# The mixer's product of e^k and v for groups 2 and 3: from VectorE in PSUM to ScalarE and GpSimd in SBUF

## The reference

```python
r = sigmoid(h @ W_r.T + b_r);  ek = exp(h @ W_k.T + b_k);  v = h @ W_v.T + b_v
td = exp(b_td);  g = exp(global_decay)
def step(carry, inputs):                    # over the 1024 tokens
    sa = ek_t * v_t + td * sa
    sb = ek_t + td * sb
    wkv = (g * ek_t * v_t + sa) / (g * ek_t + sb + EPS)
    inp_t = r_t * wkv
    mem = BETA * mem + inp_t - spike(mem - THRESH) * THRESH
    spk = spike(mem - THRESH)
```

## Time and profile before

| | |
|---|---|
| profiled execution, its own time | 566.38 us |
| its span | 564.4 us |
| median of the three runs | 566.53 us |
| mean granted TensorE clock | 0.955 of full speed |
| PE busy | 491.8 us (87%) |
| VectorE (DVE) busy | 436.7 us (77%) |
| ScalarE (ACT) busy | 348.3 us (62%) |
| GpSimd (POOL) busy | 328.7 us (58%) |

### The profile page before, as it was taken

One profiled execution on the slowest core, in us unless ns is written; L12 is line 12 of the kernel. 1 busy time (PEld: TensorE's weight loads), 2 busy tenths in 40 slices (PEclk: granted clock), 3 DMA queues, 4 the chain that ended last, 5 costly groups with the idle time before them and its releaser, 6 DMA issues. The chain is left out here.

```text
span 564.4 us, 11730 instructions
## 1 busy us (share of the span) xinstructions
PE 491.8 (87%) x4033; PEld 310.3 (55%) x4033; DVE 436.7 (77%) x1181; ACT 348.3 (62%) x1001; POOL 328.7 (58%) x255
## 2 busy tenths in 40 slices
PE   7650048999999999999989999999999989999995
PEld 6320013467777766443457777776544445667774
DVE  6899999889999875556898888885445686467775
ACT  4971004789999987632589999997555525533331
POOL 5860006999999998476999999993011274210000
PEclk9885559999999999999999999999999999999999
DMA  8400002211111112000031111111000000000000
GB/s 291 157 1 1 1 1 87 64 37 35 36 40 38 40 39 75 2 1 1 26 87 41 38 40 39 39 39 30 0 3 0 1 1 0 1 0 20 21 19 20
DMA packets 14832, 19.93 MB, mean 35 GB/s; under 512 B 2314, under 2 KB 8948, under 8 KB 14644
## 3 DMA queue, kind: packets, MB, share of 16 engines
q1 hardware_dynamic: 14484, 19.08, 12.4%
q10 hardware_dynamic: 288, 0.08, 0.1%
HBM read 8.94 MB, written 1.05 MB: 18 GB/s over the span
## 5 line engine op out<-in xcount | busy, mean ns | idle before, releaser
L516 ACT ACTIVATE prob<-psS,nmx 128x128 f32<-128x128 f32 x256 | 90.1, 378 | 17.3 <-DVE nmx L1112 17.3
L806 POOL TENSOR_TENSOR rn<-ssq,half 128x16 f32<-128x16 f32 x32 | 93.1, 2908 | 6.9 <-DVE ssq L1098 6.8
L798 POOL TENSOR_TENSOR ra<-ra,rb 128x512 f32<-128x512 f32 x64 | 80.6, 1278 | 1.0 <-DVE rb L1080 0.9
L653 POOL TENSOR_TENSOR rst<-mv,half 128x4 f32<-128x4 f32 x24 | 25.7, 1070 | 81.9 <-DVE mv L899 69.8
L1458 PE MATMUL psQK<-wqkv,hsA 128*128 128x512 f32 x128 | 61.2, 596 | 0.9 <-DVE hsA L1061 0.6
L516 ACT ACTIVATION_READ_ACCUMULATOR prob<-psS,nmx 128x1 f32 x256 | 55.4, 216 | 0.0
L1077 DVE TENSOR_TENSOR ra<-psQK,rope 128x512 f32<-128x512 f32 x64 | 43.9, 685 | 9.8 <-PE psQK L1458 9.3
L814 POOL TENSOR_TENSOR qkn<-ra,rn 128x512 f32<-128x512 f32 x32 | 49.5, 1548 | 2.5
L1112 DVE TENSOR_REDUCE nmx<-psS 128x4 f32<-128x512 f32 x64 | 41.0, 683 | 4.5 <-PE psS L1560 4.5
L634 ACT ACTIVATE gel<-psQK 128x512 f32<-128x512 f32 x32 | 19.1, 597 | 39.7 <-PE psQK L1774 39.7
L1080 DVE TENSOR_TENSOR rb<-psQK,rope 128x512 f32<-128x512 f32 x64 | 43.5, 680 | 0.0
(11 more groups left out here) (237 smaller groups left out, 1208.0 us busy)
## 6 DMA issues: line engine op xcount, KB each, us to landing
vAB<-vAB SPq DMA_DIRECT2D x62, 128.0 KB, 2.2
wqkv<-in_wqkv SPq DMA_DIRECT2D x2, 768.0 KB, 7.9
big<-in_x SPq DMA_DIRECT2D x4, 256.0 KB, 5.5
ropeb<-in_rope SPq DMA_DIRECT2D x1, 1024.0 KB, 6.5
big<-in_ew SPq DMA_DIRECT2D x2, 512.0 KB, 4.4
out<-big SPq DMA_DIRECT2D x4, 256.0 KB, 2.3
wmod<-in_wmod SPq DMA_DIRECT2D x2, 384.0 KB, 5.8
w<-in_w SPq DMA_DIRECT2D x2, 341.0 KB
```

The source lines that it names most:

```text
L516: act.activation(prob[:, k, :], psS[:, hb, c * P:(c + 1) * P], ACT.Exp, bias=nmx[:, k:k + 1], accum_out=sums[:, n % 2, k:k + 1]).then_inc( ...
L798: pool.tensor_tensor(o, o, rb[:, r], ALU.add).then_inc(s["sum_" + name], 1)
L806: pool.tensor_tensor(rn[:, :], ssq[:, :], half[:, :], ALU.pow).then_inc(s["rn_ready"], 1)
```

## The change

For groups 0 and 1 nothing changes. For groups 2 and 3 ScalarE copies v with its bias from PSUM into `ekv` in SBUF, ahead of `gek`; GpSimd multiplies it there by ek (`product`), product(2) behind quotient(0) and product(3) behind quotient(1); VectorE's multiply is left out, and its second scan and its numerator read `ekv` in SBUF instead of PSUM. VectorE's wait for the product stands behind the scan of ek.

```diff
@@ ScalarE, behind ek_ready
+                if g >= 2:
+                    act.wait_ge(s["kv_mm"], 2 * g + 2)
+                    act.activation(ekv[:, gsl(g)], psO[:, g % 2, :], ACT.Identity, bias=vec[:, V_BV:V_BV + 1]).then_inc(s["v_ready"], 1)
@@ GpSimd
+            def product(g):
+                pool.wait_ge(s["v_ready"], g - 1)
+                pool.wait_ge(s["ek_ready"], g + 1)
+                pool.tensor_tensor(ekv[:, gsl(g)], ekv[:, gsl(g)], ek[:, gsl(g)], ALU.mult).then_inc(s["ekv_ready"], 1)
...
                 if g == 1:
                     quotient(0)
+                    product(2)
                 elif g == 2:
                     quotient(1)
+                    product(3)
                     current(0)
@@ VectorE
-                ekvp = psO[:, g % 2, :]
-                dve.wait_ge(s["kv_mm"], 2 * g + 2)
+                ekvp = ekv[:, c] if g >= 2 else psO[:, g % 2, :]
                 dve.wait_ge(s["ek_ready"], g + 1)
-                dve.scalar_tensor_tensor(out=ekvp, in0=ekvp, scalar=vec[:, V_BV:V_BV + 1],
-                                         in1=ek[:, c], op0=ALU.add, op1=ALU.mult).then_inc(s["ekv_ready"], 1)
-                dve.wait_ge(s["ekv_ready"], g + 1)
+                if g < 2:
+                    dve.wait_ge(s["kv_mm"], 2 * g + 2)
+                    dve.scalar_tensor_tensor(out=ekvp, in0=ekvp, scalar=vec[:, V_BV:V_BV + 1],
+                                             in1=ek[:, c], op0=ALU.add, op1=ALU.mult).then_inc(s["ekv_ready"], 1)
+                if g < 2:
+                    dve.wait_ge(s["ekv_ready"], g + 1)
...
                 dve.tensor_tensor_scan(sbb[:, c], td, ek[:, c], ...).then_inc(s["sb_ready"], 1)
+                if g >= 2:
+                    dve.wait_ge(s["ekv_ready"], g + 1)
```

More of the change, by code:

```diff
@@ L186, in program @@
             xT_fill xT_evac
-            kv_mm num_ready ek_ready gek_ready ekv_ready sb_ready den_ready r_mm r_ready rcp_ready quot_ready cur_ready x_mixed
+            kv_mm num_ready ek_ready gek_ready ekv_ready v_ready sb_ready den_ready r_mm r_ready rcp_ready quot_ready cur_ready x_mixed
             dve dve_b act_own pool_own fallback fallback_b rope_ready tabs_phase tabs_ready z_ready hsA_ready
```

## The result

The changed kernel takes 568.79 us (median of 5 runs, 567.86 to 569.64), the kernel before 566.38 (5 runs, 565.90 to 566.98). The ratio is 1.0042, 95% interval 1.0027 to 1.0057: slower by 2.4 us, between 1.5 and 3.2.

What follows compares the result with a forecast made beforehand. Bound: the mixer's chain to VectorE's membrane passes, with GpSimd's queue 0.36 us behind VectorE. Current(0) at 37.32 plus 7.17 us of turns puts the last reciprocal at 44.5 against 41.91, +2.6: 569.1 us, range 567.4 to 570.8.

Steps and rivals of the forecast that it cites:

- Group 2's saving is eaten: VectorE, group 2: den(2) takes a turn before the numerator; reciprocal at 34.08 not 33.18, saving lost and 0.19 us more.
- Seven instructions in turn in group 3: Group 3: VectorE's two scans and numerator alternate with GpSimd's two currents, quotient(2) and den(3), 7.17 us in sum.
- rival A: Exclusion costs little for the new forms, only GpSimd's queue counts: last reciprocal +0.4 us, 566.9 us; chance 0.12.
- r is later: ScalarE: two copies of 0.66 us each delay r's release from 35.86 to 37.18, 1.32 us.
- The lead that the prediction calls a microsecond: ScalarE, group 3: V's matmul ends a microsecond ahead of the copy, so the copy does not wait.
- Product(3) hidden: GpSimd, between quotient(1) and current(0): product ends at 36.4, before 37.3, costing nothing; without that cover 1.26 us.
- Rival B: Not slower: ScalarE's copies don't reach r, current(0) stays at 36.00; without exclusion -0.9 us, 565.6 us; chance 0.05.
- a sign that the prediction itself had named for being wrong: ScalarE's r coming under 0.9 us later than before, where 1.32 was worked out.
- that case: With exclusion and undelayed r, current(0) at 36.00 plus 7.17 gives 43.2 for the last reciprocal, still +1.3 us.
- its other signs: Among them: both group 3 scans at 1.7 to 2.2 us; wrong if they keep 1.25 beside GpSimd's work.
- Rival C: TensorE's clock rises later against its work, slowing fillers after the passes: likely +1, 570.1, up to 570.8; chance 0.12.
- Rival D: VectorE's numerator at half rate with two SBUF sources: its 0.60 doubles, +0.6 us, 569.7 us; chance 0.03.

Runs made afterwards that it cites:

- with fillers: Changed kernel plus 12 filler matmuls on TensorE ahead of group 3's K matmul: 568.64 us, ratio 1.0043 to the kernel before.
- group 3 alone: Kernel before with the change made for group 3 only, group 2 left as before: 568.00 us, ratio 1.0024.
- second profile: Profiled execution of the changed kernel run again without edit, beside the kernel before; that run took 569.10 us, ratio 1.0036.
- side work: Kernel before plus ScalarE's two copies and GpSimd's two products, VectorE keeping its multiply and reading PSUM: 568.78 us, ratio 1.0029.
- group 2 alone: Kernel before with the change made for group 2 only, group 3 left as before: 566.98 us, ratio 1.0004.
- changed with den(3) second: Changed kernel with GpSimd's group 3 denominator sum moved between current(0) and current(1): 566.67 us, ratio 1.0009 to the kernel before.
- changed with den(3) first: Changed kernel with GpSimd's group 3 denominator sum moved ahead of current(0), current(1) and quotient(2): 566.33 us, ratio 1.0000 to the kernel before.
- before with den(3) first or second: Kernel before with group 3's denominator sum ahead of current(0), current(1) and quotient(2) (first), 566.69 us, or between current(0) and current(1) (second), 565.40 us.

## Why the prediction was right

The mechanism came as forecast: turns between the two engines, behind a later r. The size is 568.79 against 569.1, but that closeness is in part luck. The last reciprocal was to come 2.6 us later; it came 1.70, 2.88 and 2.63 later in the three profiles of the changed kernel (the third with fillers), and one term of the sum was too large while something that is not in it, the clock, worked the other way.

- *Group 2's saving is eaten.* Numerator 1.57 us (about 1.6 said), den(2) 2.03 (2.0), third reciprocal at 33.99 (34.08), where it would have been near 33.2 without the turns.
- *Seven instructions in turn in group 3.* 7.27 us in the first profile, 7.27 with group 3 alone and 7.20 with fillers (7.17 said). After a release a GpSimd instruction ended 1.05 to 1.13 us later (1.05), a scan 1.08 to 1.10 (1.08), the numerator 0.54 to 0.55 (0.60). Only the second profile of the changed kernel, with r behind the first scan, had 6.22. A line that had only one SBUF tensor became the form of line 945 and behaved like it; rival A is refuted by the kernel with the product in SBUF.
- *r is later.* Right in kind, mis-sized: 1.32 us said. Counted from line 393 for group 2, r(0) took 11.80 or 11.81 us in the four profiles without a copy, 12.37 with one (group 3 alone), 12.94 to 12.96 with two in the three where TensorE's clock stayed high. So a copy costs 0.57 or 0.58 us, as ScalarE's next instruction starts 0.59 after it (0.66 said), and the two cost 1.15. Where the clock fell it took 13.1 to 14.1 us, which the sum did not have. Then the copies did wait, against the prediction: in the second profile the copy of group 3 stood 0.33 us for V's matmul. The lead that the prediction calls a microsecond was 0.65 us before (31.73 to 32.38). And the whole mixer can be a microsecond early, as in the first profile.
- *Product(3) hidden.* Only if r is late. In the first profile r was there at 35.93, and current(0), which could have started 0.14 us later, waited for product(3) until 36.38, 0.31 us more.
- *Rival B.* In the first profile r(0) came only 0.07 us later than before on the clock of the program, a sign that the prediction itself had named for being wrong. The time did not follow B, since the turns took 7.27 us from current(0) on. So without a late r the change lost 1.70 us there, where the prediction had 1.3 for that case. Of its other signs the scans of group 3 hold in part only: 1.48 and 2.23 us in the first profile (1.7 to 2.2 said), 1.18 and 1.25 in the second, where no GpSimd instruction lay beside the first scan and the second scan came ahead of current(0), which stood still instead.
- *Rival C*: the ten fillers after the passes took 2.33 us in the changed kernel (2.43 before), no loss.
- *Rival D*, the halved rate that the Trainium skill gives (Vector Engine (DVE) Microarchitecture Reference, Points that are easy to get wrong) for this form: the numerator ended 0.55 us after its release, as line 1163's 0.752 had said; the measurement decides, and there is no halving here.

The Trainium skill says that, of a VectorE instruction with two SBUF inputs and a GpSimd instruction that reads SBUF, the second to issue blocks until the first finishes (SBUF — State Buffer, section Summary: rules for kernel authors). The traces agree: in the changed kernel's first profile the second scan, issued at 38.66 beside current(1), ended 1.08 us after it. What the runs add is the order behind it: with both sides waiting in line, the turns alternated in each case shown here.

Each part costs something by itself: copies alone 1.1 us (0.3 to 1.6), SBUF reads alone 1.2 (0.7 to 2.0), the whole change 2.0 to 2.4 by its three ratios. A split of the whole into shares is not shown: the kernel with copies and products but no SBUF reads was already 2.2 us over before by the medians (0.8 to 2.5). What the prediction had not seen is that within single executions the parts replace each other: in the first profile r came early and more turns were taken, in the second it came late, VectorE waited 3.61 us and fewer were.

## What to carry to other kernels

Here, moving the product out of PSUM made VectorE's instructions on it take turns with GpSimd. Before such a move, count, for every GpSimd instruction between the last free point and the end, who stands beside it and how many tensors it reads from SBUF. Before work is taken off the engine that looks full, look at the queue of the engine that releases its last wait: here one instruction moved two places forward was worth 0.9 us (0.3 to 1.6), and taking the multiplies away, with all that it needed, cost 2.0 to 2.4. And when such a move is made, look at what it pushes back, since the same conflict can wait there.

## What the hardware showed that was not expected

TensorE's granted clock early in the program differs between executions of one and the same kernel, and in five profiles it fell back to the lower level behind a wait. The table by stretches (busy us and instructions of each engine, then the granted clock, DMA share and GB/s) of the changed kernel in its first profile:

```profile
22.00:24.00 2.00, 0.75 (x7) 0.52 (x5) 1.97 (x3) 2.00 (x4) 1.96 (x2) 1.00 0.01 4
```

and in its second:

```profile
22.00:24.00 2.00, 2.00 (x9) 1.51 (x7) 1.40 (x2) 1.65 (x3) 0.92 (x1) 0.57 0.01 4
30.00:31.00 1.00, 0.68 (x1) 0.32 (x2) 1.00 (x2) 0.27 (x1) 0.00 (x0) 0.77 0.00 0
31.00:32.00 1.00, 1.00 (x2) 0.34 (x1) 1.00 (x1) 0.00 (x0) 0.92 (x1) 0.50 0.00 0
```

1.00 is 2.4 GHz, 0.50 is 1.2 GHz. In the second the matmuls before 24 us ran mostly at the low level, and behind the 2.58 us without a matmul ahead of 30.32 the clock fell back to it for group 3's K matmul, which took 1.89 us and not 1.12. With the fillers it stayed at 1.00 from 26 to 34 us. The wait alone does not decide it. Seven profiles have this wait at 2.58 or 2.59 us. In five the clock fell within or behind group 3's K matmul (changed kernel's second, copies alone, side work, group 2 alone, changed with den(3) second). In two it stayed at 1.00 (changed kernel's first, changed with den(3) first), and those are the two that had 1.00 already from 22 to 24 us. In the five profiles with a wait of 2.00 or 2.01 us (before, product in SBUF only, group 3 alone, before with den(3) first or second) it had not fallen by 34 us.

The kernel before itself spread from 564.98 to 568.48 us over the 35 runs beside the first four kernels, more than the effect of most edits here; only medians over many runs tell them apart. Whether the early clock makes that spread was not tried; of the three profiled executions with 1.00 from 22 to 24 us, two are the fastest of their kernel (567.86 and 565.36 us) and one is its median (565.40).
